# Self-attention stage of a Perceiver kernel: value product with its operands swapped, one output product, row sums in two steps

## The chip, the cores and the metric

The kernel runs on one core of one Trainium2 chip. Its measure is the device time of one execution in microseconds (us), as the median of several runs. The engines of the core are TensorE (PE in the profile; PEld is its weight load), VectorE (DVE), ScalarE (ACT), GpSimd (POOL) and SyncE (SP), which here only starts transfers.

## What is computed

Inputs: x is 128 batches x 32 queries x 128 channels, the context 128 x 257 x 128. Everything is float32. Three blocks follow one another, each added to its input:

```
x = x + cross_attention(layernorm(x), ctx, ctx, mask)        # 16 heads of 8 channels
x = x + self_attention(layernorm(x))
x = x + mixture_of_experts(layernorm(x))                      # 4 layers, 4 experts, the best 2
```

The change is in the second:

```
qkv    = x @ W_qkv + b_qkv                       # B, N = 128, 32
energy = einsum('bqhe,bkhe->bqhk', q, k)
attn   = softmax(energy, axis=-1) / sqrt(128)
out    = einsum('bihv,bvhd->bihd', attn, v)
return out.reshape(B, N, 128) @ W_out + b_out
```

Each softmax row has 32 entries, the positions of one batch.

## The kernel before, in words

The program has three stages, each a block in which every engine has its own written list of instructions, with semaphores between them. Stage 1 is the cross attention (the first 492 us), stage 2 the self attention (492 to 637 us), stage 3 the experts (the rest).

**Stage 2.** The 4096 tokens are 32 tiles of 128 (four batches of 32 tokens), and 8 blocks of four tiles. A step works on one block, and in it four places w = 0 to 3 each work on one tile of each of five phases, side by side: at place w of step s, scores are made for tile 4s+w+2 (`sc`), row sums for tile 4s+w+1 (`nm`), the transpose for tile 4s+w (`tr`), the value product for the tile before (`pv`), and the output product for the one before that (`y`). Beside them, the projections of block s+2 (`f`) are spread over the places: at w = 0 its normalised tokens `xm` are transposed, at w = 1 and 2 its queries and keys are projected, at w = 3 its values. The heads stand as 4 groups (G) of 4 (GH).

The order in which each engine takes the work of one place is fixed by the program text:

- TensorE: scores (L1279), projection (L1287, L1292 or L1295), transpose (L1302), value product (L1314), output product (L1322).
- VectorE: row maximum (L1226), difference (L1229), at w = 3 the normalising of block s+3 (L141), at w = 1 and 2 the low half of queries or keys (L1239), row sum (L1244), reciprocal (L1246), output added to `xs` (L1250), its statistics (L1254).
- ScalarE: the copy of the projection out of PSUM (L1164, L1173, L1177), the transposed probabilities `pT` (L1182), the value product `oT` (L1187), the exponential (L1195).
- GpSimd: at w = 0 the bias added to a block of `xs` (L1145), then the probabilities times the reciprocals (L1150).
- SyncE starts the transfers: it places the values V2 (L164), writes the queries and keys of a block to DRAM (L148) and its values (L152), and then reads queries (L157) and keys (L160) back in the layout of the scores, and last loads two parts of the experts' weights (L1121, L1122). The scores at w = 2 are the first of a new block and wait for these reads.

Waits that the prediction uses: the low halves of the queries have to be done (`c_lo`) before the keys are projected, as both go through one PSUM bank:

```python
                            if f and w in (1, 2):
                                pe.wait_ge(c_xTc, f.n + 1)
                                wait(pe, c_lo, 2 * f.n + w - 1)
```

The value product puts the four heads of a group on the partitions, so its output holds for every head the columns of all heads, of which only its own are wanted; four copies of W_out (`WoutM`), each with the rows of the other heads at zero, pick them in four output products that add up. These copies are made by VectorE in `prepare` at the start of stage 2, with `bv2R` (the value bias, scaled), the last six layer-norm deviations, and `boutR`.

**Stage 1** is a list of slots s from -22 to 133, one batch each. At s = 2 it loads the weights of the self attention; from FIRST = 113 it already makes the projections of the first block.

## Time and profile before

| | |
|---|---|
| median of 3 runs | 1492.02 us (1490.94 to 1494.69) |
| the profiled execution: its own time, and its span | 1491.5 us, 1489.3 us |
| granted TensorE clock, mean over the span | 0.957 |
| busy over the span: TensorE, VectorE, ScalarE, GpSimd | 89%, 82%, 74%, 47% |
| stage 2, of the span | 492 to 637 us |

The span runs from the first to the last instruction. Engine times in the profile are busy times of an engine, and each row names the line of the kernel, the engine, the tile written and the tiles read. A timeline row begins with the start of the instruction and its duration, both in us.

### The profile page before, as it was taken

To read this page: it belongs to the slowest core of one execution; us is meant where nothing else is said; L and a number is where in the kernel's file an instruction comes from. 1 tells how busy PE (TensorE), PEld (TensorE's weight loads), DVE (VectorE), ACT (ScalarE), POOL (GpSimd) and SP (SyncE) were. 2 spreads that over 40 slices of the span, in tenths; PEclk is the share of its full clock that TensorE was granted. 3 is DMA by queue.
4 is the path that set the end of the run, shared out by engine and by line. 5 is a ranking of instruction groups with operands and counts; after the bars stand their busy time and mean duration, and the time that the engine had idled before them with its cause. 6 is when DMAs were issued, how large, how long until landed. Compare 5 with 4: busy or idle time off the path is not lost.

```text
span 1489.3 us, 46126 instructions
## 1 busy us (share of the span) xinstructions
PE 1326.8 (89%) x15863; PEld 1010.5 (68%) x15863; DVE 1217.0 (82%) x3478; ACT 1101.6 (74%) x1844; POOL 702.9 (47%) x464
## 2 busy tenths in 40 slices
PE   5898999999978699969887898999999999898988
PEld 3676777777857599936665666766676666666666
DVE  6799999998997788778788777787877878787885
ACT  2698999999978255538777677777787778677776
POOL 7276777777768433223332233443444344333323
PEclk9999999999987599979999899999999999999999
DMA  5975766666642478400000000000000000000000
GB/s 154 233 194 158 190 178 185 187 172 188 180 135 65 122 195 198 112 1 2 2 0 0 0 1 2 0 0 0 0 0 0 0 0 0 2 7 14 7 14 15
DMA packets 196200, 108.46 MB, mean 73 GB/s; under 512 B 89740, under 2 KB 194028, under 8 KB 196076
## 3 DMA queue, kind: packets, MB, share of 16 engines
q1 hardware_dynamic: 122032, 84.65, 20.4%
q10 hardware_dynamic: 74044, 22.17, 6.8%
q8 instruction: 76, 1.25, 0.4%
q14 instruction: 48, 0.39, 0.1%
HBM read 67.62 MB, written 39.03 MB: 72 GB/s over the span
## 4 chain that ended last, share of the span: by engine, by line
DVE 20%; PE 14%; issue 13%; ACT 5%; DVEq 2%; ACTq 0%
PE pair L1734 7%; PE pair L1716 5%; DVE hs L1647 4%; ACT gf L1589 3%; ACT gh L1594 2%; DVE xc L1621 2%; DVE gl L1633 1%; DVE rs L50 1%; DVE rs L52 1%; DVE st L1612 1%; PE pair L1746 1%; DVE rs L48 1%; DVE rs L37 1%; DVE mv L1616 1%; DVE sel L1699 1%
## 5 line engine op out<-in xcount | busy, mean ns | idle before, releaser
L1576 POOL TENSOR_TENSOR gl<-gf,gh 128x1024 f16<-128x1024 f32 x128 | 292.6, 2286 | 543.9 <-ACT gh L1594 543.9
L1589 ACT ACTIVATE gf<-pair,b1c 128x512 f32<-128x512 f32 x512 | 326.6, 679 | 149.1 <-PE pair L1716 148.9
L1734 PE MATMUL pair<-w2p,gh 128*128 (+1 forms) x4096 | 366.9, 222 | 12.0 <-DVE gl L1633 12.0
L1734 PE MATMUL pair<-w2p,gl 128*128 (+1 forms) x2048 | 358.1, 222 | 0.0
L1734 PEld LDWEIGHTS pair<-w2p,gh 128*128 128x128 f16 x4096 | 326.5, 99 | 37.7 <-issue 8.4
L407 POOL TENSOR_TENSOR pl<-p,ph 128x1024 f16<-128x1024 f32 x128 | 272.7, 2131 | 125.5 <-ACT ph L464 125.2
L1716 PE MATMUL pair<-xh,w1p 128*128 128x512 f16 x1024 | 327.1, 381 | 3.6 <-DVE w2p L1363 2.9
L1594 ACT ACTIVATE gh<-gf 128x1024 f16<-128x1024 f32 x256 | 270.6, 1057 | 25.2 <-ACT gf L1589 2.0
L1633 DVE TENSOR_TENSOR gl<-gf,gh 128x1024 f16<-128x1024 f32 x128 | 169.0, 1320 | 122.7 <-ACT gh L1594 120.6
L1734 PEld LDWEIGHTS pair<-w2p,gl 128*128 128x128 f16 x2048 | 203.5, 99 | 0.0
L1716 PE MATMUL pair<-xl,w1p 128*128 128x512 f16 x512 | 195.0, 381 | 0.0
L463 ACT ACTIVATE p<-pair 128x512 f32<-128x512 f32 x256 | 158.8, 620 | 32.6 <-PE pair L868 31.1
L1716 PEld LDWEIGHTS pair<-xh,w1p 128*128 (+1 forms) x1024 | 100.6, 98 | 111.8 <-issue 5.0
L464 ACT ACTIVATE ph<-pair 128x512 f16<-128x512 f32 x256 | 161.2, 630 | 0.0
L770 DVE TENSOR_REDUCE mx<-pair 128x4 f32<-128x1024 f32 x128 | 154.7, 1208 | 1.3 <-PE pair L841 0.2
L1647 DVE SCALAR_TENSOR_TENSOR hs<-pair,comb,hs 128x128 f32 (+1 forms) x512 | 142.6, 337 | 6.9 <-PE pair L1734 6.9
L891 PE MATMUL pair<-VX,ph 128*128 128x36 f16 x1024 | 92.5, 180 | 7.9 <-DVE lsb L608 5.1
L891 PEld LDWEIGHTS pair<-VX,ph 128*128 128x128 f16 x1024 | 84.1, 97 | 18.8 <-issue 14.8
L841 PE MATMUL pair<-KS,QS 97*128 97x256 f16 x512 | 79.4, 278 | 14.7 <-DVE mx L770 13.3
L892 PE MATMUL pair<-VX,ph 128*128 128x36 f16 x1024 | 91.8, 180 | 0.0
L893 PE MATMUL pair<-VX,pl 128*128 128x36 f16 x1024 | 91.8, 180 | 0.0
L821 PE MATMUL pair<-cT,WkT 128*128 128x512 f32 x128 | 72.0, 645 | 19.1 <-DVE VX L797 9.2
(232 smaller groups left out, 2518.8 us busy)
## 6 DMA issues: line engine op xcount, KB each, us to landing
KS<-k_parts_dram SPq DMA_DIRECT2D x64, 384.0 KB, 4.5
k_parts_dram<-kh SPq DMA_DIRECT2D x64, 256.0 KB, 3.3
cx<-in_ctx_dram ACTq DMA_DIRECT2D x30, 512.0 KB, 4.4
k_parts_dram<-kl SPq DMA_DIRECT2D x64, 128.0 KB, 3.5
w1p<-in_L_ffn_w_dram SPq DMA_DIRECT2D x8, 512.0 KB, 6.1
w2p<-in_L_ffn_w_dram SPq DMA_DIRECT2D x8, 512.0 KB, 8.0
QS<-q_parts_dram ACTq DMA_DIRECT2D x128, 24.0 KB
Q<-q_parts_dram SPq DMA_DIRECT2D x32, 96.0 KB
```

What stands on the lines that cost most here:

```text
L407: pool.tensor_tensor(pl[n % 4][:, :, :], p32[n % 2][:, :, :], ph[n % 4][:, :, :], ALU.subtract).then_inc(pl_done, 1)
L463: act.activation(p32[n % 2][:, c, :], TB[:, c * 512:(c + 1) * 512], ACT.Exp)
L464: act.activation(ph[n % 4][:, c, :], TB[:, c * 512:(c + 1) * 512], ACT.Exp).then_inc(t_read[c], 1)
L770: dve.tensor_reduce(mx[n // PB % 2][:, :, n % PB], RB[:, :].rearrange("p (g k) -> p g k", g=G), AX.X, ALU.max).then_inc(r_read, 1)
L891: pe.matmul(o, p_hi, hi, start=(c == 0), stop=False)
L1576: pool.tensor_tensor(gl[u.m2][:, 0:h, :], gf[u.m2][:, 0:h, :], gh[u.m2][:, 0:h, :], ALU.subtract).then_inc(d_loP, 1)
L1589: act.activation(gf[u.m2][:, c, :], hb[c][:, :], ACT.Gelu, scale=1.0 / WS, bias=b1c[:, u.step.expert(u.e), c]).then_inc(d_g, 1)
L1594: act.activation(gh[u.m2][:, c - 1:c + 1, :], gf[u.m2][:, c - 1:c + 1, :], ACT.Copy).then_inc(d_hi, 1)
L1633: dve.tensor_tensor(gl[u.m2][:, h:FC, :], gf[u.m2][:, h:FC, :], gh[u.m2][:, h:FC, :], ALU.subtract).then_inc(d_loD, 1)
L1647: dve.scalar_tensor_tensor(t, yb[v.m2][:, k * D:(k + 1) * D], comb[v.step.m2][:, k, v.e:v.e + 1], t, ALU.mult, ALU.add).then_inc(d_acc, 1)
L1716: last = pe.matmul(hb[c][:, :], w1p[:, u.step.expert(u.e), part, c * P:(c + 1) * P].rearrange("p a f -> p (a f)"), x[k][u.step.m2][:, :], ...
L1734: last = pe.matmul(yb[v.m2][:, t * D:(t + 1) * D], g[:, c, t * P:(t + 1) * P], w2p[:, le, part, c, :].rearrange("p a h -> p (a h)"), start ...
```

## The change

It has four parts.

- The value product takes the transposed probabilities as weights and V2 as the moving operand. Its output has queries and heads on the partitions and (group, head, channel) along the row. ScalarE copies it whole (`of`); GpSimd then takes, for each of the four heads of a group, the quarter of 32 partitions and of its own channels and multiplies it by the reciprocal row sums (`on2`, four instructions a tile); VectorE transposes the 128 x 128 result in 32 x 32 squares (`oT2`). One output product with the whole of W_out takes the place of four.
- The probabilities are no longer multiplied by the reciprocals, and the transpose on TensorE waits for the exponential alone. The row sum is made in two steps: GpSimd adds the right half of each row of 32 to the left half (`hs2`), VectorE sums the 16 columns left.
- The normalising of block s+3 moves from VectorE to ScalarE, with scale `rs2` and bias `nb2` (a new small VectorE product, twice in the program).
- `WoutM`, `rowsel` and `sel3` go. W_out is loaded in another order of rows, by four transfers (four more for the value bias in place of one), and scaled by ScalarE in stage 1, as is `bv2R`; the product of the value bias and its sum with `boutR` also move to stage 1.

```diff
@@ stage 1, SyncE, s == 2
-                        sp.dma_start(Wout[:, :], W_out).then_inc(c_w, 16)
+                        for j in range(GH):
+                            sp.dma_start(Wout[GD * j:GD * (j + 1), :],
+                                         W_out.rearrange("(g j d) n -> j g d n", j=GH, d=DH)[j]).then_inc(c_w, 16)
+                            sp.dma_start(bv2_c[GD * j:GD * (j + 1), :],
+                                         b_qkv[2 * D:3 * D].rearrange("(g j d a) -> j g d a", j=GH, d=DH, a=1)[j]).then_inc(c_w, 16)
...
@@ stage 1, ScalarE
+                    if s == FIRST - 4:
+                        act.wait_ge(c_w, CW)
+                        act.activation(Wout[:, :], Wout[:, :], ACT.Copy, scale=float(D) ** -0.5).then_inc(c_wm, 1)
+                        act.activation(bv2R[:, :], bv2_c[:, 0:1].broadcast_to((P, D)), ACT.Copy).then_inc(c_wm, 1)
...
@@ stage 1, VectorE
                     if s == FIRST - 2:
...
+                        dve.scalar_tensor_tensor(nb2[:, 0:EARLY], mv2[:, 0:EARLY, 0], -1.0, rs2[:, 0:EARLY], ALU.mult, ALU.mult).then_inc(c_ln, 1)
...
+                    if s == FIRST + 5:
+                        dve.wait_ge(c_w, CW)
+                        dve.wait_ge(c_b, 1)
+                        dve.tensor_tensor(boutR[:, :], WB[0][:, 0:D], boutR[:, :], ALU.add).then_inc(c_wm, 1)
...
@@ stage 1, TensorE
+                    if s == FIRST + 4:
+                        pe.wait_ge(c_wm, 2)
+                        pe.wait_ge(c_vn, 1)
+                        pe.matmul(WB[0][:, 0:D], bv2R[:, :], Wout[:, :], start=True, stop=True).then_inc(c_b, 1)
...
@@ stage 2, GpSimd
                             if f and w == 0:
 
-                                pool.wait_ge(c_wm, 6)
+                                pool.wait_ge(c_wm, 3)
+                                wait(pool, c_on, GH * (4 * st.s - 1))
+                                wait(pool, c_hf, 4 * st.s + 1)
...
                             if nm is not None:
                                 i = (w + 1) % 4
-                                pool.wait_ge(c_rc, nm + 1)
-                                pool.tensor_tensor(pr[i][:, :, :, :], pr[i][:, :, :, :],
-                                                   rc2[i][:, :, :].unsqueeze(3).broadcast_to((P, PB, G, SQ)),
-                                                   ALU.mult).then_inc(c_nrm, 1)
+                                pool.wait_ge(c_exp, nm + 1)
+                                wait(pool, c_on, GH * (nm - 2))
+                                wait(pool, c_sum, nm - 1)
+                                pool.tensor_tensor(hs2[(w + 1) % 2][:, :, :, :], pr[i][:, :, :, 0:SQ // 2], pr[i][:, :, :, SQ // 2:SQ],
+                                                   ALU.add).then_inc(c_hf, 1)
+                            if pv is not None:
+                                i, r = (w + 1) % 2, (w - 1) % 4
+                                pool.wait_ge(c_rc, pv + 1)
+                                pool.wait_ge(c_oc, pv + 1)
+                                pool.wait_ge(c_bias, f.n + 1 if f else NBLK)
+                                pool.wait_ge(c_hf, NT if nm is None else nm + 1)
+                                wait(pool, c_oT, pv - 1)
+                                for h in range(GH):
+                                    own = slice(SQ * h, SQ * (h + 1))
+                                    pool.tensor_tensor(on2[i][own, :, :, :], of[i][own, :, :, h, :],
+                                                       rc2[r][own, :, :].unsqueeze(3).broadcast_to((SQ, PB, G, DH)),
+                                                       ALU.mult).then_inc(c_on, 1)
...
@@ stage 2, ScalarE
+                            if w == 3 and st.block(3):
+                                b = st.block(3)
...
+                                wait(act, c_xT, b.n)
+                                for k in range(4):
+                                    t = bass.ds(4 * b.n + k, 1)
+                                    act.activation(xm[:, k, :], xs[:, t, :].rearrange("p a c -> p (a c)"), ACT.Identity,
+                                                   scale=rs2[:, t], bias=nb2[:, t]).then_inc(c_xm, 1)
...
                             if pv is not None:
                                 i = (w + 1) % 2
                                 act.wait_ge(c_o, pv + 1)
-                                wait(act, c_y, pv - 1)
-                                act.activation(oT2[i][:, :, :, :].rearrange("p h b q -> p b h q"),
-                                               bank[6][:, :].rearrange("p (b h q) -> p b h q", b=PB, h=GH),
+                                wait(act, c_on, GH * (pv - 1))
+                                act.activation(of[i][:, :, :, :, :].rearrange("p b g h d -> p (b g h d)"), bank[6][:, :],
                                                ACT.Copy).then_inc(c_oc, 1)
...
@@ stage 2, VectorE
                     def prepare():
-                        dve.tensor_scalar(bv2R[:, :], bv2_c[:, 0:1].broadcast_to((P, D)), float(D) ** -0.5, None, ALU.mult).then_inc(c_wm, 1)
-                        for j in range(GH):
-
-                            dve.tensor_scalar(WoutM[:, j, :], Wout[:, :], rowsel[:, j:j + 1], float(D) ** -0.5,
-                                              ALU.mult, ALU.mult).then_inc(c_wm, 1)
...
-                        dve.wait_ge(c_b, 1)
-                        dve.tensor_tensor(boutR[:, :], bank[7][:, 0:D], boutR[:, :], ALU.add).then_inc(c_wm, 1)
+                        dve.scalar_tensor_tensor(nb2[:, late], mv2[:, late, 0], -1.0, rs2[:, late], ALU.mult, ALU.mult).then_inc(c_ln, 1)
...
-                            if w == 3 and st.block(3):
-                                normalise(st.block(3))
...
-                                dve.wait_ge(c_exp, nm + 1)
-                                dve.tensor_reduce(sm2[i][:, :, :], pr[i][:, :, :, :], AX.X, ALU.add).then_inc(c_sum, 1)
+                                dve.wait_ge(c_hf, nm + 1)
+                                wait(dve, c_on, GH * (nm - 3))
+                                dve.tensor_reduce(sm2[i][:, :, :], hs2[(w + 1) % 2][:, :, :, :], AX.X, ALU.add).then_inc(c_sum, 1)
                                 dve.wait_ge(c_sum, nm + 1)
                                 dve.reciprocal(rc2[i][:, :, :], sm2[i][:, :, :]).then_inc(c_rc, 1)
+                            if pv is not None:
+                                i = (w + 1) % 2
+                                dve.wait_ge(c_on, GH * (pv + 1))
+                                wait(dve, c_y, pv - 1)
+                                dve.transpose(out=oT2[i][:, :, :].rearrange("p b q -> p (b q)"),
+                                              in_=on2[i][:, :, :, :].rearrange("p b g d -> p (b g d)")).then_inc(c_oT, 1)
...
@@ stage 2, TensorE
                             if tr is not None:
-                                pe.wait_ge(c_nrm, tr + 1)
+                                pe.wait_ge(c_exp, tr + 1)
...
                                     last = pe.matmul(bank[6][:, b * P:(b + 1) * P],
+                                                     pT[(w + 1) % 2][:, b * P:(b + 1) * P],
                                                      V2[m][:, t * PB + b, :, :].rearrange("k g c -> k (g c)"),
-                                                     pT[(w + 1) % 2][:, b * P:(b + 1) * P], start=True, stop=True)
+                                                     start=True, stop=True)
...
                             if y is not None:
-                                pe.wait_ge(c_oc, y + 1)
+                                pe.wait_ge(c_oT, y + 1)
                                 wait(pe, c_yr, y)
-                                for h in range(GH):
-                                    last = pe.matmul(bank[7][:, 0:D], oT2[w % 2][:, h, :, :].rearrange("p b q -> p (b q)"),
-                                                     WoutM[:, h, :], start=(h == 0), stop=(h == GH - 1))
-                                last.then_inc(c_y, 1)
+                                pe.matmul(bank[7][:, 0:D], oT2[w % 2][:, :, :].rearrange("p b q -> p (b q)"), Wout[:, :],
+                                          start=True, stop=True).then_inc(c_y, 1)
```

## Rows read from the trace of the kernel before

**Rows 1.** Windows, one step: length, PE, PEld, DVE, ACT, POOL, clock, DMA share, GB/s.
```profile
525.00:541.30 16.30, 16.30 (x163) 15.03 (x162) 13.64 (x31) 9.13 (x17) 5.43 (x5) 1.00 0.74 194
```

**Rows 2.** Timeline of TensorE, one place (w = 1) and the next steps' scores.
```profile
561.59 1.11 PE L1279 MATMUL pair<-K,Q 96*128 96x32 f16 x16
...
562.55 1.10 PE L1292 MATMUL pair<-xmT,Wqkv 128*128 128x512 f32 x2
...
563.49 0.60 PE L1302 MATMUL pair<-ident,pr 128*128 128x128 f32 x4
...
563.93 1.06 PE L1314 MATMUL pair<-pT,V 128*128 128x128 f32 x8
...
564.82 1.06 PE L1322 MATMUL pair<-WoutM,oT 128*128 128x128 f32 x8
...
565.72 1.11 PE L1279 MATMUL pair<-K,Q 96*128 96x32 f16 x16
...
577.84 1.12 PE L1279 MATMUL pair<-K,Q 96*128 96x32 f16 x16
```

**Rows 3.** Timeline of VectorE in the same place (w = 1).
```profile
562.74 0.69 DVE L1226 TENSOR_REDUCE mx<-pair 128x16 f32<-128x512 f32 x1
...
563.46 0.69 DVE L1229 TENSOR_TENSOR dif<-pair,mx 128x512 f32<-128x512 f32 x1
...
565.17 0.68 DVE L1244 TENSOR_REDUCE sm<-pr 128x16 f32<-128x512 f32 x1
...
566.07 0.29 DVE L1250 TENSOR_TENSOR xs<-pair,xs 128x128 f32 x1
...
566.50 0.29 DVE L1254 BATCH_NORM_STATS2 st<-xs  x1
```

**Rows 4.** Timeline of place w = 3: value projection, its copy, normalising, next copy.
```profile
570.80 1.14 PE L1295 MATMUL pair<-Wqkv,xmT 128*128 128x128 f32 x8
...
572.06 0.60 ACT L1177 ACTIVATE vn<-pair 128x512 f32<-128x512 f32 x1 [1.80 <-PE pair L1295]
...
572.32 1.11 DVE L141 TENSOR_SCALAR xm<-xs,mv,rs 128x128 f32 x4
572.55 0.59 ACT L1182 ACTIVATE pT<-pair 128x512 f32<-128x512 f32 x1
```

**Rows 5.** Instructions near to the new ones, by line: duration min/median/max in ns.
```profile
L1150 POOL TENSOR_TENSOR pr<-pr,rc x32: 1046/1047/1052, 509.5 to 628.9; 128x512 f32<-128x512 f32 x32
...
L415 POOL TENSOR_TENSOR tl<-VL,plast x32: 432/442/465, 66.2 to 480.4; 128x144 f32<-128x144 f32 x32
...
L1145 POOL TENSOR_TENSOR xs<-xs,boutR x8: 1262/1270/1278, 502.0 to 591.7; 128x512 f32<-128x512 f32 x4, 128x512 f32 x4
...
L652 DVE STREAM_TRANSPOSE onT<-on x64: 220/230/247, 78.7 to 490.1; 128x64 f32<-128x64 f32 x64
```

**Rows 6.** Timeline, stage 3: sixteen ScalarE instructions of the new kind, in one run.
```profile
651.83 6.25 ACT L1407 ACTIVATE hs<-xs,nb,rs 128x128 f32<-128x128 f32 x16
```

**Rows 7.** Timeline of the start of stage 2.
```profile
493.44 5.57 DVE L1207 TENSOR_SCALAR WoutM<-Wout,rowsel 128x128 f32<-128x128 f32 x4
...
498.03 0.69 ACT L1173 ACTIVATE qkh<-pair,bqk_c 128x512 f16<-128x512 f32 x1 [2.17 <-PE pair L1292]
...
501.75 0.74 DVE L1239 SCALAR_TENSOR_TENSOR qkl<-pair,bqk_c,qkh 128x512 f16<-128x512 f32 x1
...
502.64 2.04 PE L1292 MATMUL pair<-xmT,Wqkv 128*128 128x512 f32 x2 [3.71 <-DVE qkl L1239]
```

**Rows 8.** Timeline: key loads, waiting scores; page: issues of a like load.
```profile
510.85 0.36 SPq L160 DMA_DIRECT2D K<-k_parts_dram  x1
...
516.75 1.17 PE L1279 MATMUL pair<-K,Q 96*128 96x32 f16 x16 [0.51 <-DMA K<-k_parts_dram]
...
574.91 0.36 SPq L160 DMA_DIRECT2D K<-k_parts_dram  x1
...
KS<-k_parts_dram SPq DMA_DIRECT2D x64, 384.0 KB, 4.5
```

More of the change, by code:

```diff
@@ L94, in build @@
         ident16 = sb(whole, "ident16", [P, P], F16)
-        rowsel = sb(whole, "rowsel", [P, GH], F32)
         boR = sb(whole, "boR", [P, D], F32)
@@ L102, in build @@
         bv2_c = sb(whole, "bv2_c", [P, 1], F32)
+        bv2R = sb(whole, "bv2R", [P, D], F32)
+        c_wm, c_b = sem("c_wm"), sem("c_b")
+        CW = 16 * (4 + 2 * GH)
         boutR = sb(whole, "boutR", [P, D], F32)
@@ L109, in build @@
         mv2 = sb(whole, "mv2", [P, NT, 2], F32)
-        rs2, rw2, rt2 = (sb(whole, f"rs2_{i}", [P, NT], F32) for i in range(3))
+        rs2, rw2, rt2, nb2 = (sb(whole, f"rs2_{i}", [P, NT], F32) for i in range(4))
         xm = sb(whole, "xm", [P, 4, D], F32)
@@ L1018, in build @@
             NBLK = NT // 4
-            WoutM = sb(S, "WoutM", [P, GH, D], F32)
-            bv2R = sb(S, "bv2R", [P, D], F32)
             qkh = [qkh[0], [sb(S, f"qkh1{k}", [P, 4 * P], F16) for k in range(2)]]
```

58 lines of the change are left out of this document (22 added, 36 removed).

## The prediction

> **What bounds it now.** I read the windows first. The self-attention stage takes 145 us of the span, from 492 to 637, and in its middle a step of four tiles takes 16.3 us in which TensorE is busy all the time, at the full granted clock (1.0, the 2.4 GHz level), VectorE for 84%, ScalarE 56%, GpSimd 33% [rows 1]. So TensorE bounds this part, and the other stages see the change only in small edits. The timeline then shows what one place consists of. From start to start: scores 0.96, projection 0.94, transpose 0.44, value product 0.89, output product 0.90, together 4.13 us, and the next place begins [rows 2]. At w = 0 the short transposes of `xm` stand in for a projection, so that four places make 577.84 - 561.59 = 16.25 us. VectorE's place runs maximum, difference, [low half], row sum, reciprocal, addition, statistics [rows 3], and ends ahead of TensorE's. Its lead is what the change spends.
>
> **The output product** goes from four to one: 3/4 of 0.90 = 0.67 us a tile off the engine that bounds, and 16.25 - 4 x 0.67 = 13.6 us a step, if TensorE went on without a pause. The value product keeps its shape with the operands swapped: nothing.
>
> **VectorE** loses the normalising (1.11 us a step [rows 4]) and half of each row sum. The row sum is 0.68 for 512 elements [rows 3], a transpose 0.23 for 64 [rows 5]: about 1.0 ns an element, so half a row sum is 0.42. It gains the transpose. At 128 elements that is some 0.30, and 0.24 from start to start, as an instruction starts up to 0.08 before the last one's end. In the order maximum, difference, row sum, reciprocal, transpose, addition, statistics, from start to start, a place then costs it 0.72 + 0.61 + 0.44 + 0.24 + 0.24 + 0.43 + 0.22 = 2.9 us, and 0.67 more at w = 1 and 2: 12.9 a step, under 13.6.
>
> **GpSimd** loses 1.05 us a tile and gains a half sum and four quarters. Multiplications take 1.047 us for 512 elements and 0.442 for 144 [rows 5]: 1.64 ns an element on a fixed 0.205. A quarter has 128 elements a row: 0.415. The half sum has 256: 0.63, or with the slower addition of L1145 (1.27 for 512) up to 0.77; I take 0.70. What four quarters take together, which I call T, no row shows. From above: one after another, 4 x 0.415 = 1.66. From below: all side by side, each on its own 32 partitions, little over 0.5. I take the fixed parts one after another and one element part, 4 x 0.205 + 0.21 = 1.03, as instructions on separate partitions need not share the work by element but do share the way into the engine. Between the ends 0.5 and 1.66 that is the middle, and both ends stay in the range.
>
> The Trainium skill's page GPSIMD Engine Reference, section Instruction dispatch, says that each core of the engine serves its own 16 partitions and starts the next instruction as soon as its own share is done. By it the quarters overlap, and T would lie at or under my value. No row of before has GpSimd instructions on parts of the partitions that could show it.
>
> **The new waits** are what decides. VectorE's transpose stands in its queue behind the reciprocal and waits for GpSimd's quarters, these for ScalarE's copy `of`, that for the value product of the same place. Behind the waiting transpose queue the addition, the statistics, and the next place's maximum, difference and low half; and TensorE may not project the keys before the low half of the queries (L1291). The second new load is on ScalarE at w = 3: four normalising instructions, between the copy `vn` and `pT` and `of`. Sixteen like them took 6.25 us [rows 6], so four take 1.6, and `of` comes that much later. GpSimd then still has the bias (1.24) before the next quarters, at w = 0. This closes a ring once a step. From the start of the value projection: to `vn` 1.26 [rows 4], `vn` 0.49, normalising 1.6, `pT` 0.49, `of` 0.65 with the signal, quarters T, bias 1.24, half sum 0.70, quarters T + 0.05, transpose 0.24, addition 0.43, statistics 0.22, maximum 0.72, difference 0.61 [rows 3], low half 0.75 [rows 7] + 0.05, keys' projection 0.94, transpose 0.44, value product 0.89, output product 0.23, scores 0.96 [rows 2]. The sum is 12.96 + 2T. With T = 1.03 a step lasts 15.0 us, not 13.6; with T = 1.66 it lasts 16.3, as now.
>
> A second ring runs through the transfers: from the first scores of a block (565.72) to `vn` (572.06) 6.34, less 0.67 for one output product; from there to the issue of the key load at 574.91 2.85; to its landing 4.5, as for stage 1's load of the same size, up to 5.9, as the scores at 516.75 waited for a load issued at 510.85 [rows 8]. That is 13.0 to 14.4. It sits close under the first ring, and the DMA share, 0.74 of 16.3 us [rows 1], becomes 0.8.
>
> **The sum.** Five full steps (blocks 2 to 6) at 16.25 - 15.0 = 1.2: -6.2 us. The start of the stage: `WoutM` holds VectorE 5.6 us, and the low half that was due at 498.77, when `qkh` ended, begins at 501.75, with TensorE idle 3.7 for it [rows 7]. Between the end of `WoutM` at 499.0 and that low half lie 2.7 us of small instructions; with `WoutM` gone they are over by 497, and the low half begins when due: -3.0, and the transpose no longer waits for GpSimd's product, -0.2. The last eight tiles have no projections: 4.13 - 0.94 = 3.2 us a place now, bound by VectorE's 2.9 afterwards: -2.4, less 1.0 for the longer way out after the last value product (quarters, transpose): -1.4. Stage 1 gets two copies on ScalarE (0.39 each by rows 6), `nb2` (some 0.2), one addition on VectorE (0.29) and one small product: 0 to 1.9, and I take +0.8, as these engines are dense there. The six more transfers at s = 2 come far ahead of their use, and SyncE's loads of keys run slots ahead: nothing. Together -6.2 - 3.2 - 1.4 + 0.8 = -10.0. The profiled execution took 1491.5 us (span 1489.3 and 2.2 around it), so 1481.5; the median of the runs is 0.5 above it: 1482.0.
>
> Another rule that bears on GpSimd's new work is in SBUF — State Buffer of the Trainium skill, section Who interferes with whom: a VectorE instruction with one SBUF input outside the two-port modes does not contend with GpSimd. The new sum and transpose are of that kind. If it failed, they would wait out each half sum, 0.7 us a tile, and the step would be 16 us or more.
>
> **Rivals.**
> - *The quarters run one after another.* T = 1.66, ring 16.3: the steps give nothing. Left are -3.2 at the start, -0.8 at the end (a way out 0.6 longer), +0.8: -3.2, 1488.8 us, within 0.3%. For it: consecutive instructions on all partitions show no overlap worth naming. Against: those share all partitions.
> - *GpSimd becomes a loss.* One mechanism: an instruction on 32 partitions with eight-element runs costs 0.6 us, T = 2.4, the ring 17.8: five steps at +1.5, -3.2, +0.3 at the end, +0.8: +5.4, 1497.4 us. It decides from T = 1.7 a step, and over the whole from about 2.0. The dearest comparable row, L1145, would make a quarter 0.5 (T = 2.0) [rows 5].
> - *TensorE stays the bound.* T near 0.5 puts the ring at 14.0, the transfers at 13.0 to 14.4; with both at their lower end 13.6 to 14.0 a step: five steps at -2.4, -3.2, -1.7, +0.4: -16.5, 1475.5 us.
> - *The output product does not matter*, because steps are held by the transfers: landing at 5.9 under more load, 14.4 or more, and SyncE's issues late. The time is near my forecast; only the wait is another.
>
> **Chances.** Forecast, with the fourth rival: 0.55 (1478 to 1486). One after another: 0.23. Loss: 0.10. TensorE bound: 0.08. The rest, 0.04, is a wait I haven't seen, most likely a loss. A measurement of this kernel can tell 0.3%, 4.5 us. Faster by more (under 1487.5): 0.55 + 0.08 + a third of the second: 0.70. Within 0.3%: 0.18. Slower: 0.12. The range, 1475 to 1490.5, leaves out the loss and little else.
>
> **What would show it.** The output product's row at a quarter of its count, TensorE busy some 90% of a step instead of all of it. Steps of 15.0 us in the starts of the scores, four places apart. The wait of VectorE's transpose for GpSimd, longest after w = 3; TensorE waiting for the low half before the keys' projection and for VectorE's addition before the output product. The four quarters' length from first start to last end: under 1.0 confirms the forecast or better, 1.6 the first rival, 2.0 the second. First scores of a block waiting for the key load would show the fourth. At the start, the second projection some 3 us sooner. I am wrong if steps stay at 16.2 with T near 1, if GpSimd's instructions lengthen VectorE's, or if stage 1 grows by more than 2 us.

## The result, and the profile after

The changed kernel took 1516.8 us (median of 4, 1514.3 to 1519.8) against 1492.4: a ratio of 1.016, 95% interval 1.014 to 1.019. I had said 1482.0, and faster at 0.70. The profiled execution took 1519.8 us (span 1518.0), 28.7 more than before's span. The starts of three instructions, each from its row by line, split that: the maximum of stage 1, that of stage 2, and stage 3's first hidden product. I put my terms beside them. Each difference is one profiled execution against one.

| part of the span | before | after | difference | my term |
|---|---|---|---|---|
| start to first maximum of stage 1 | 36.1 | 41.5 | +5.4 | 0 |
| to its last maximum | 426.9 | 428.1 | +1.2 | +0.8 |
| to stage 2's first, and its first four tiles | 54.9 | 55.4 | +0.5 | -3.2 |
| five steps (525.0 to 611.3) | 81.3 | 86.3 | +5.0 | -6.2 |
| last tiles, to the first hidden product | 68.2 | 68.0 | -0.2 | -1.4 |
| stage 3's hidden products, first to last | 811.2 | 828.5 | +17.3 | 0 |
| the rest | 10.6 | 10.2 | -0.4 | 0 |

Windows of one step after (columns as in [rows 1]):
```profile
541.82:559.26 17.44, 15.83 (x140) 14.18 (x139) 12.09 (x31) 10.81 (x22) 10.60 (x21) 0.90 0.72 185
```
Against [rows 1] TensorE has become an engine with gaps, VectorE is busy for 12.1 us (12.9 forecast), and GpSimd has doubled. A step takes 86.3 / 5 = 17.26 us; before 16.27. Groups by line in stage 2 (busy, mean ns | idle before, releaser):
```profile
L1173 POOL TENSOR_TENSOR on<-of,rc 32x128 f32<-32x128 f32 x128 | 51.3, 401 | 44.9 <-ACT of L1219 28.4 <-DVE rc L1267 6.4 <-POOL hs L1162 1.9
L1162 POOL TENSOR_TENSOR hs<-pr 128x256 f32<-128x256 f32 x32 | 23.5, 735 | 4.8 <-ACT pr L1226 2.3
L1343 PE MATMUL pair<-Wout,oT 128*128 128x128 f32 x64 | 14.3, 307 | 14.2 <-DVE xs L1277 14.2
L1265 DVE TENSOR_REDUCE sm<-hs 128x16 f32<-128x256 f32 x32 | 13.1, 410 | 2.2 <-POOL hs L1162 1.9
L1209 ACT ACTIVATE xm<-xs,rs,rs 128x128 f32 (+1 forms) x28 | 11.5, 483 | 7.3 <-PEq L295 7.3
L1272 DVE STREAM_TRANSPOSE oT<-on 128x128 f32<-128x128 f32 x32 | 10.0, 312 | 33.3 <-POOL on L1173 33.3
```
The single instructions came out as sized: quarter 0.401 us (0.415), half sum 0.735 (0.70), row sum 0.410 (0.42). The two waits I named are there: VectorE's transpose for GpSimd, 33.3 us over 32 tiles, and the output product for VectorE's addition. What I had wrong is how four quarters add up. Timeline of GpSimd, ScalarE, VectorE and TensorE around w = 3:
```profile
597.34 1.64 ACT L1209 ACTIVATE xm<-xs,rs,rs 128x128 f32 x4
598.89 0.58 ACT L1214 ACTIVATE pT<-pair 128x512 f32<-128x512 f32 x1
599.37 0.58 ACT L1219 ACTIVATE of<-pair 128x512 f32<-128x512 f32 x1
600.16 1.83 POOL L1173 TENSOR_TENSOR on<-of,rc 32x128 f32<-32x128 f32 x4 [2.09 <-DVE rc L1267]
602.02 0.31 DVE L1272 STREAM_TRANSPOSE oT<-on 128x128 f32<-128x128 f32 x1 [1.88 <-POOL on L1173]
602.12 1.27 POOL L1155 TENSOR_TENSOR xs<-xs,boutR 128x512 f32<-128x512 f32 x1
602.33 0.29 DVE L1277 TENSOR_TENSOR xs<-pair,xs 128x128 f32 x1
602.77 0.46 PE L1343 MATMUL pair<-Wout,oT 128*128 128x128 f32 x2 [1.55 <-DVE xs L1277]
603.35 0.75 POOL L1162 TENSOR_TENSOR hs<-pr 128x256 f32<-128x256 f32 x1
604.35 1.82 POOL L1173 TENSOR_TENSOR on<-of,rc 32x128 f32<-32x128 f32 x4 [0.26 <-POOL hs L1162]
606.20 0.31 DVE L1272 STREAM_TRANSPOSE oT<-on 128x128 f32<-128x128 f32 x1 [1.21 <-POOL on L1173]
```
This is my ring, link by link: normalising, `pT`, `of`, quarters, bias, half sum, quarters, transpose. Four quarters take 1.83 us from first start to last end: no overlap at all, and 0.07 between each pair. (The first bracket names `rc`, but the reciprocals of this tile had been made two places earlier; the quarters waited for `of`, which ended at 599.95.) The ring's sum with T = 1.83 is 12.96 + 3.66 = 16.6. Part of what it lacks stands in these rows: from `of` to the quarters 0.79 us (I had 0.65), from the first quarters to the bias 1.96 (T is 1.83), and from the half sum to the next quarters 1.00 (0.70 and 0.05).

**The start.** VectorE and GpSimd, 25 to 37 us, first in the kernel before:
```profile
27.76 2.91 POOL L382 MEMSET VX<- 128x640 f16 x1
28.52 2.24 DVE L742 CAST ident<-ident 128x128 f16<-128x128 f32 x1
30.27 0.41 POOL L383 MEMSET sel<- 128x16 f32 x1
30.76 0.27 POOL L385 TENSOR_SCALAR_AFFINE_SELECT sel<-sel 128x16 f32<-128x16 f32 x1
31.37 3.51 POOL L391 MEMSET Q<- 96x4096 f32 x1
```
and after:
```profile
27.35 2.90 POOL L386 MEMSET VX<- 128x640 f16 x1
28.10 7.38 DVE L747 CAST ident<-ident 128x128 f16<-128x128 f32 x1
29.83 3.83 POOL L387 MEMSET Q<- 96x4096 f32 x1
33.59 1.81 POOL L388 MEMSET V<- 128x2048 f32 x1
```
Before, VectorE's cast ends at 30.76, between the selector's memset and its first select, which waits for that memset: the short `sel3` instructions, with the waits between them, let it through. Without them each of three memsets begins before the one ahead has ended (29.83 against 30.25), and the cast is held until 35.5.

**Stage 3**, VectorE's normalisation `xc` and GpSimd's low half `gl`, a quick block and the next, a slow one:
```profile
1014.03 1.12 DVE L1641 TENSOR_SCALAR xc<-hs,mv,rs 128x128 f32 x4
1014.93 3.35 POOL L1596 TENSOR_TENSOR gl<-gf,gh 128x1024 f16<-128x1024 f32 x1 [3.14 <-ACT gh L1614]
1015.21 0.66 PE L1766 MATMUL pair<-ident,xc 128*128 128x128 f32 x4 [1.03 <-DVE xc L1641]
...
1038.07 3.01 DVE L1641 TENSOR_SCALAR xc<-hs,mv,rs 128x128 f32 x4
1038.87 2.13 POOL L1596 TENSOR_TENSOR gl<-gf,gh 128x1024 f16<-128x1024 f32 x1 [3.05 <-ACT gh L1614]
1041.13 1.12 PE L1766 MATMUL pair<-ident,xc 128*128 128x128 f32 x4 [3.02 <-DVE xc L1641]
...
1090.07 3.44 POOL L1596 TENSOR_TENSOR gl<-gf,gh 128x1024 f16<-128x1024 f32 x1 [3.05 <-ACT gh L1614]
```
If `gl` begins 0.90 us after `xc`, it is the one held; at 0.80, the fourth `xc`, which starts 0.77 us after the first, is held for 1.9 us. It is a race: in block 17 `gl` began 0.81 after `xc` (last row) and `xc` still won, as `gl`'s 3.44 us show. From one block's `xc` to the next is 24.0 us in the first case, 27.2 in the second. Windows of the two blocks:
```profile
1014.03:1038.07 24.04, 23.01 (x261) 16.50 (x260) 19.16 (x63) 19.07 (x27) 9.76 (x4) 1.00 0.00 0
1038.07:1065.23 27.16, 24.14 (x261) 17.63 (x260) 20.56 (x62) 18.99 (x27) 8.54 (x4) 0.94 0.00 0
```
So the 3.1 us more have two parts. TensorE waits 3.02 us for `xc` and not 1.03, 2.0 more; and from the end of that wait or just behind it the granted clock, 1.00 all through the quick block, is at half (1.2 GHz) for 3.4 us, TensorE being busy 1.1 us longer with the same 261 instructions. Every slow block has such a spell. Blocks 11 to 24 hold six slow ones (27.1 to 28.7 us) after, none (23.9 each) before: 22 us, of which blocks 4 to 10, 5 us shorter than before, give some back.

The Trainium skill's page SBUF — State Buffer, section Who interferes with whom, says that VectorE's copies, casts and tensor_scalars may take a port pair which they share with GpSimd, and that whoever comes first shuts the other out for the whole instruction. Both places agree with it (the cast held for 7.38 us, the fourth `xc` for 1.9); I had used that section for the new instructions of stage 2 alone, where it held too (row sum 0.410, transpose 0.312).

### The profile page after: what moved, and what is told of

It reads as the page before. It is cut to its first block, busy times and chain, and to the rows that moved or that the text cites. A ratio compares the mean times of both kernels' runs of the same rounds, so it can differ in the third digit from the quotient of the medians.

```text
span 1518.0 us, 46101 instructions
## 1 busy us (share of the span) xinstructions
PE 1328.8 (88%) x15671; PEld 1006.3 (66%) x15671; DVE 1213.2 (80%) x3478; ACT 1114.1 (73%) x1874; POOL 736.9 (49%) x589
## 4 chain that ended last, share of the span: by engine, by line
DVE 20%; PE 15%; issue 12%; ACT 5%; DVEq 1%; ACTq 0%
PE pair L1754 7%; PE pair L1736 6%; DVE hs L1667 4%; ACT gf L1609 3%; DVE xc L1641 2%; ACT gh L1614 2%; DVE rs L50 1%; DVE gl L1653 1%; DVE rs L52 1%; PE pair L1766 1%; DVE st L1632 1%; DVE rs L48 1%; DVE rs L37 1%; DVE mv L1636 1%; PE pair L1743 1%
## 5 line engine op out<-in xcount | busy, mean ns | idle before, releaser
L1596 POOL TENSOR_TENSOR gl<-gf,gh 128x1024 f16<-128x1024 f32 x128 | 285.8, 2233 | 568.1 <-ACT gh L1614 568.1
L1754 PE MATMUL pair<-w2p,gh 128*128 (+1 forms) x4096 | 373.1, 224 | 12.1 <-DVE gl L1653 12.1
L1754 PE MATMUL pair<-w2p,gl 128*128 (+1 forms) x2048 | 363.8, 223 | 0.0
L1754 PEld LDWEIGHTS pair<-w2p,gh 128*128 128x128 f16 x4096 | 330.8, 100 | 38.5 <-issue 9.5
L1653 DVE TENSOR_TENSOR gl<-gf,gh 128x1024 f16<-128x1024 f32 x128 | 163.9, 1280 | 126.7 <-ACT gh L1614 124.6
L893 PE MATMUL pair<-VX,ph 128*128 128x36 f16 x1024 | 92.4, 180 | 10.6 <-DVE lsb L608 5.2
```

What stands on the lines that cost most here:

```text
L893: pe.matmul(o, p_hi, hi, start=(c == 0), stop=False)
L1596: pool.tensor_tensor(gl[u.m2][:, 0:h, :], gf[u.m2][:, 0:h, :], gh[u.m2][:, 0:h, :], ALU.subtract).then_inc(d_loP, 1)
L1653: dve.tensor_tensor(gl[u.m2][:, h:FC, :], gf[u.m2][:, h:FC, :], gh[u.m2][:, h:FC, :], ALU.subtract).then_inc(d_loD, 1)
L1754: last = pe.matmul(yb[v.m2][:, t * D:(t + 1) * D], g[:, c, t * P:(t + 1) * P], w2p[:, le, part, c, :].rearrange("p a h -> p (a h)"), start ...
```

## The experiments

Steps are the starts of stage 2's maxima, from the fifth to the 25th tile, divided by five; stage 3 is from first to last hidden product; `xc` its mean. Medians are of 4 to 10 runs beside as many or more of the kernel before (1489.7 to 1491.2).

| run | median us | ratio, 95% | step us, clock there | stage 3 us | `xc` ns |
|---|---|---|---|---|---|
| before | | | 16.27, 1.00 | 811.2 | 355 |
| changed | 1516.8 | 1.014-1.019 | 17.26, 0.90 | 828.5 | 445 |
| 1 fillers | 1509.8 | 1.012-1.016 | 17.20, 0.90 | 825.6 | 431 |
| 2 late transpose | 1507.0 | 1.009-1.012 | 16.98, 0.92 | 823.2 | 416 |
| 3 one multiply | 1494.9 | 0.999-1.004 | 14.45, 1.00 | 819.8 | 416 |
| 4 bias later | 1508.3 | 1.008-1.014 | 16.96, 0.89 | 824.9 | 430 |
| 5 selector last (before) | 1495.7 | 1.001-1.004 | 16.27, 1.00 | 811.8 | 355 |
| 6 stage 3 later (before) | 1503.3 | 1.006-1.010 | 16.30, 1.00 | 822.3 | 356 |
| 7 normalise on VectorE | 1512.9 | 1.009-1.018 | 19.10, 0.85 | 814.1 | 370 |
| 8 reordered, first | 1510.6 | 1.009-1.016 | 18.26, 0.88 | 826.1 | 429 |
| 9 normalise earlier | 1492.0 | 1.000-1.003 | 16.72, 0.96 | 805.9 | 356 |
| 10 TensorE kept busy | 1517.2 | 1.014-1.024 | 17.33, 0.98 | 826.9 | 444 |
| 11 reordered, second | 1477.3 | 0.989-0.993 | 15.02, 1.00 | 807.2 | 355 |
| 12 reordered, third | 1478.3 | 0.991-0.994 | 15.90, 0.95 | 806.3 | 356 |
| 13 full multiply | 1493.3 | 1.001-1.004 | 17.50, 0.98 | 806.9 | 356 |
| 14 second, one multiply | 1468.7 | 0.982-0.987 | 14.67, 1.00 | 807.5 | 356 |
| 15 stage 3 kept apart | 1562.6 | 1.046-1.051 | 17.04, 0.92 | 874.7 | 342 |
| 16 second, kept apart | 1545.8 | 1.034-1.040 | 14.75, 1.00 | 878.0 | 343 |
| 17 small op first | 1571.4 | 1.049-1.056 | 17.24, 0.90 | 881.9 | 686 |
| 18 second, small op first | 1540.6 | 1.031-1.036 | 15.03, 1.00 | 875.7 | 681 |

**The start: runs 1 and 5.** Run 1 puts the selector's instructions back:
```diff
+                pool.memset(sel3[:, :, :], 1.0).then_inc(a_fill, 1)
...two affine selects with their waits, ahead of Q2's memset
```


> The changed kernel with the three small GpSimd instructions that made the row selector (memset and two affine selects, 128x16 each) put back between the memset of VX and those of Q2 and V2; nobody reads their result. Theory: the changed kernel loses 5.4 us in its first 42 us, because VectorE's copies into the 16-bit identity and wo_p (2.2 us before, 7.3 us after) are held up while GpSimd's memsets follow one another without a gap; the three small instructions gave VectorE its gap. Then the first running maximum of stage 1 comes back from 41.5 us to about 36.1 us, and the time falls from 1516.8 to about 1511.5 us, give or take what stage 3 does with the shift. Rival: the start grew for another reason (loads, the order of the queues), and the time stays within 1 us of 1516.8.

> The kernel before with one thing moved: the three small GpSimd instructions that make the row selector come after the memsets of Q2 and V2 and not before them, as if they weren't there for those who wait at that point. Theory: the gap that they leave between GpSimd's memsets is what lets VectorE's copies through; without it the first maximum of stage 1 moves from 36.1 us to about 41.5 us, and the time grows by about 5.4 us or, if stage 3 is sensitive to when it begins, by up to 20 us. Rival: the order of memsets doesn't matter, the first maximum stays at 36 us and the time at 1490.4.

First maximum at 35.9 us in run 1; 41.0 in run 5, whose median is 5.0 us over its neighbours' of before. Both theories held: 5 us of the loss come from three tiny instructions, and the waits between them, that went.

**The ring: runs 3, 2 and 4.** Run 3:
```diff
-                                for h in range(GH):
-                                    own = slice(SQ * h, SQ * (h + 1))
+                                for h in range(1):
+                                    own = slice(0, P)
```


> The changed kernel with one GpSimd multiplication over 128 partitions (the first quarter of each row, 128x128) in place of the four over 32; it leaves out three of four diagonal quarters of the value product, and so computes something else. Theory: the four instructions run one after another (0.40 us each, 1.83 us together), and one takes 0.4 to 0.7 us; a step falls from 17.3 us to between 13.6 and 14.5 us, where TensorE or the transfers take over, and the time to about 1497 us. Rival: the steps are set by something other than the quarters (ACT's normalising, the split row sum, the transpose): the steps stay above 16 us and the time above 1508.

Its row by line (ns min/median/max):
```profile
L1173 POOL TENSOR_TENSOR on<-of,rc x32: 405/408/410, 521.0 to 622.5; 128x128 f32<-128x128 f32 x32
```
128 partitions take as long as 32. T falls by 1.83 - 0.41 = 1.42, and my ring, which holds T twice, asks for 2.84 us a step; measured 17.26 - 14.45 = 2.81. That fits my ring's slope, its constant 0.64 short both times (16.62 for 17.26, 13.78 for 14.45), but the agreement to 0.03 is in part luck. A step of run 3:
```profile
541.20:555.60 14.40, 14.05 (x138) 12.53 (x138) 11.60 (x31) 10.40 (x21) 5.81 (x9) 1.00 0.85 230
```
TensorE is busy 14.05 of 14.40 us there, so the ring hardly sets this step any more. What is shown is that the quarters are in the ring of the changed kernel, and are worth at least 2.8 us of its step.

Run 2 moves the transpose behind the next place's difference, run 4 the bias behind the quarters.

> The changed kernel with VectorE's transpose of a tile moved behind the running maximum and difference of the next place, so that GpSimd's four quarters (1.83 us together) have a whole place to finish in. Theory: the quarters stand in the ring that sets the step, value product, ACT's eviction, quarters, transpose, addition, statistics, next maximum; with the transpose later the step falls from 17.3 us to about 15.0, the granted clock in stage 2 rises from 0.85 towards 1.0, and the time falls by 10 to 14 us, to about 1505. Rival: GpSimd's own order (bias addition, half sum, quarters) holds the place at w=0 whatever VectorE does, steps stay above 16.5 and the time falls by 4 us at most.

> The changed kernel with GpSimd's addition of the output bias (1.27 us, once in a step at w=0) moved behind the four quarters of its place. Theory: in that place GpSimd runs bias, half sum and quarters without a gap, with VectorE's transpose waiting at their end, so the step falls by 0.8 to 1.25 us, to about 16.3, and the time by 4 to 6 us, to about 1511.5. Rival: the place only shifts its wait to the next one, and the time falls by less than 1.5 us.

Steps of 16.98 and 16.96: each alone gives 0.3 us, far under what I expected. In both, ScalarE's 1.6 us still delays the quarters of w = 3; in run 2 the half sum that waits behind bias and quarters then holds VectorE up to 2.0 us.

**The normalising: runs 7, 8 and 9.** Run 7 gives it back to VectorE, behind the difference; run 8 joins runs 1, 2, 4 and moves it behind the exponential of w = 3; run 9 changes the changed kernel by this alone:
```diff
-                            if w == 3 and st.block(3):
+                            if w in (1, 2) and st.block(3):    # placed behind the exponential
...
-                                for k in range(4):
+                                for k in (2 * w - 2, 2 * w - 1):
```


> The changed kernel with the normalisation of a block (four 128x128) back on VectorE (1.1 us) from ACT (1.64 us). Theory: on ACT it stands ahead of the eviction of the transposed probabilities and of the value product in the place w=3, and so delays the quarters there by 1.5 us; on VectorE it only takes 1.1 us at a point where that engine would wait for GpSimd: the step falls from 17.3 us to 15.8 to 16.5, and the time by 4 to 8 us. Rival: VectorE has no such room, the step stays within 0.3 us of 17.3 and the time within 2 us.

> The changed kernel with four moves together: fillers back between GpSimd's memsets, VectorE's transpose in the next place, GpSimd's bias addition behind the quarters, and ACT's normalisation behind the exponential of its place. The same instructions, in another order. Theory: each of the moves takes one piece of work out of the ring that sets the step; together the step falls from 17.3 us to 14 to 14.6 us, the clock in stage 2 stays at 1.00, and the time is 1483 to 1490 us with stage 3 in its slow course (825 us) and 1470 to 1476 with the quick one (811 us). Rival: the four quarters hold the step by themselves (GpSimd busy 4 times 2.6 us and 1.3 us, 11.7 us in a step, but always behind ACT's eviction), steps stay above 16 us and the time above 1500.

> The changed kernel with ACT's normalisation of the next block (four of 0.48 us at w=3, ahead of both evictions) moved behind the exponentials of w=1 and w=2, two tiles in each. Theory: in the changed kernel TensorE waits about 1.5 us once in a step, at w=3, because ACT's 1.6 us stand ahead of the two evictions there, the quarters start that much later and everything behind them too; after that wait the granted clock falls to half for 3.4 us, which costs as much again. Without it the step falls from 17.3 us to 14.5 to 15.8 and stage 2's clock rises from 0.90 to 0.95 or more; time 1503 to 1511. Rival: the 1.6 us only move to another place (as when they were put behind the exponential of w=3, where TensorE then waited 1.6 us for them), and the step stays above 16.8.

Run 7's theory and run 8's fell: steps of 19.1 and 18.3 us. In both TensorE waits for the normalised block at w = 0, in run 8 1.6 us each time (group of its transposes):
```profile
L1316 PE MATMUL pair<-ident,xm 128*128 128x128 f32 x20 | 4.2, 344 | 8.1 <-ACT xm L1233 8.1
```
Early enough, in run 9, the same instructions give 0.5 us a step, not the 1.5 to 2.8 that I expected, 2.5 in the last tiles (25.7 to 23.3), and a quick stage 3. The median falls by 25 us. The profiled execution, the fastest of the ten, is 33 us shorter than the changed kernel's, 22.6 of them in stage 3.

**Is it the clock? Run 10.**
```diff
+                            if f and w == 3:
+                                pe.wait_ge(c_lo, 2 * f.n + 2)
+                                for b in range(6):
+                                    pe.transpose(bank[1][:, (b % 4) * D:(b % 4 + 1) * D], xmT[:, (b % 4) * P:(b % 4 + 1) * P], ident[:, :])
```


> The changed kernel with six further TensorE transposes (128x128 of xmT into a bank that is free there, about 0.22 us each, 1.3 us together, nobody reads them) between the value product and the output product of w=3, where TensorE otherwise waits about 1.5 us. Theory: it is the wait that brings the granted clock down to half for 3.4 us in each step; with work in its place the clock stays at 1.00 in stage 2 and, though TensorE has 1.3 us more to do in a step, the step falls from 17.3 us to 15.5 to 16.5 us. Rival: the clock doesn't follow from that wait, or the slow 3.4 us cost nothing since the ring through GpSimd sets the step: the step stays at 17.3 us or grows.

The clock came back to 0.98 and the step stayed at 17.33: the rival. In the changed kernel TensorE waits 1.3 to 1.7 us in each of the five steps, and behind it the granted clock drops to half (1.2 GHz) for 3.4 us, but in stage 2 that time is hidden: the ring through GpSimd is what lasts. The wait isn't at w = 3, as I had written, but at w = 0, ahead of the output product (602.77 in the rows above). There run 10's transposes only make TensorE come later, and it still waits 0.7 to 1.4 us. Behind it, where the changed kernel works at half clock, run 10 mostly has the full clock, and waits 0.8 us at w = 1 and 0.9 at w = 2 (none, and at most 0.5, in the changed kernel). Its extra transposes, 0.8 us, are work that the changed kernel hasn't, so it bounds what the clock costs and doesn't measure it.

**A better order: runs 11 to 14.** Run 11 is run 8 with run 9's normalising; run 12 the same with the bias ahead of the quarters. Run 14 is run 11 with one multiplication, run 13 with one over 128 x 512 and four transposes:
```diff
+                                pool.tensor_tensor(on2[i][:, :, :, :, :].rearrange("p b g h d -> p (b g) (h d)"), of[i]..., rc2[r]..., ALU.mult)
...
+                                for h in range(GH):
+                                    last = dve.transpose(out=oT2[i][own, :, :]..., in_=on2[i][own, :, :, h, :]...)
```


> The changed kernel with fillers between GpSimd's memsets, VectorE's transpose in the next place, GpSimd's bias addition behind the quarters, and ACT's normalisation behind the exponentials of w=1 and w=2. It differs from the first reordered kernel in the place of the normalisation alone. Theory: that kernel's step of 18.3 us came from TensorE's waiting 1.6 us for the normalised block and the clock dips behind it; here nothing in the ring is left that needs more than TensorE's 13.6 us, the step is 13.8 to 14.8 us with the clock at 1.00, and the time 1470 to 1488 us, by the course of stage 3. Rival: TensorE waits somewhere else, dips stay, and the step stays above 16 us.

> As the second reordered kernel, but with GpSimd's bias addition left ahead of half sum and quarters at w=0. Theory: with the transpose in the next place, GpSimd's 1.3 us at w=0 still delay the quarters of that place, VectorE's transpose behind them and the half sum: the step is 0.3 to 1.3 us longer than in the second reordered kernel. Rival: there is enough slack by now and the two steps agree within 0.2 us.

> The second reordered kernel with one GpSimd multiplication of 128x128 (0.41 us) in place of the four; it leaves out three of four diagonal quarters, and so computes something else. Theory: with everything else out of the ring, the four instructions still hold the step at 15.0 us, and without 1.4 us a tile it falls to what TensorE has to do, 13.6 to 14.0 us. Rival: what holds the 15.0 us is the way of queries, keys and values through memory: the step stays within 0.4 us of 15.0.

> The second reordered kernel (1477.3 us, step 15.0 us) with GpSimd's four quarter multiplications replaced by one over all 128 partitions and 512 columns, and VectorE's one transpose by four over 32 partitions that take the quarters. Theory: a GpSimd instruction's time follows its columns, not its partitions (0.40 us for 32x128, 0.41 for 128x128), so one of 128x512 takes 1.05 us against 1.83 for the four, and four transposes of 32 partitions take 0.25 to 0.6 us more on VectorE than the one: the step falls by 0 to 0.8 us, time 1473 to 1477. Rival: VectorE's four transposes take as long each as the one (0.31 us, 1.2 together), its 0.9 us more in a place take up what GpSimd saves, and the step grows by up to 1 us.

Run 11 takes 15.0 us a step, a little over what I expected, and 1477.3 us: 0.991 of the kernel before, with the change's own instructions. Run 12's step is 0.9 longer. Run 14, which computes something else, shows that the quarters have left the ring: 0.35 us less, not 2.8, and the same stage 2 gave 14.75 and 15.03 in runs 16 and 18. What holds 14.7 us was not isolated, but run 14's trace has the sign of its rival: the five steps alternate between 14.0 and 15.0 to 15.4 us, and the one wait of TensorE over 1 us in two of the long ones (1.1 and 1.5) is for the key load. Windows of 20 tiles of run 11:
```profile
517.10:592.20 75.10, 71.84 (x684) 63.39 (x685) 60.91 (x151) 52.04 (x98) 51.39 (x102) 0.98 0.84 211
```
Run 13's rival held, and more: a transpose of 32 partitions takes 0.300 us, as long as one of 128, and the step grew by 2.5 us where the rival had up to 1.
```profile
L1266 DVE STREAM_TRANSPOSE oT<-on 32x128 f32<-32x128 f32 x80 | 24.0, 300 | 0.8
L1170 POOL TENSOR_TENSOR on<-of,rc 128x512 f32<-128x512 f32 x20 | 21.0, 1048 | 42.7 <-DVE oT L1266 26.1 <-ACT of L1217 16.6
```

**Stage 3: runs 6, 15 to 18.** Run 6 puts eight VectorE instructions between the stages of the kernel before. Runs 15 and 16 add a wait in stage 3, runs 17 and 18 a small instruction:
```diff
+                            if f and e == 0:
+                                pool.wait_ge(d_x, 4 * f.n + 4)          # runs 15, 16
...
+                            if f and e == 0:                            # runs 17, 18
+                                pool.tensor_tensor(spare[:, :], gf[u.m2][:, 0, 0:64], gh[u.m2][:, 0, 0:64], ALU.subtract)
```


> The kernel before, with eight further VectorE instructions (128x128, about 0.34 us each, some 2.7 us together) between stage 2 and stage 3, written to a tile that nobody reads; stages 1 to 3 themselves are untouched. The changed kernel's stage 3 is 17 us longer than before's (first to last hidden product 828.5 us against 811.2) though its code is the same. Theory: stage 3 has a quick and a slow course, in the slow one VectorE's normalisation xc meets GpSimd's low half gl again and again and TensorE's clock dips every 51 us, and which course it takes hangs on the instant at which it begins; then this kernel's stage 3 also comes out at 815 to 830 us and the time rises by clearly more than the 2.7 us put in, to 1495 to 1510. Rival: stage 3 is slower for something that the change leaves behind (the place of tiles in memory, the activation unit's state): stage 3 stays at 811 us and the time at 1490 to 1493.5.

> The changed kernel with one wait more, in stage 3: at the first expert of a block GpSimd starts its low half gl only when VectorE has finished the normalisation xc of the next block. Stages 1 and 2 are the changed kernel's. Theory: stage 3's slow blocks (27.2 us against 23.9) are those in which VectorE's xc is held for 1.9 us by GpSimd's gl, after which TensorE waits and its clock falls to half for 3.4 us; kept apart, the blocks 11 to 24 all take 23.9 us, stage 3 takes 806 to 812 us against 828, and the time falls from 1516.8 to about 1500 us. Rival: the held xc is a consequence of the clock's dips and not their cause, or the added wait delays GpSimd's own work: stage 3 stays at 820 us or more.

> The second reordered kernel with the same wait in stage 3. Its profiled stage 3 already ran in the quick course (807.2 us, no block above 24 us among blocks 11 to 24). Theory: nothing to gain there, the time stays within 3 us of 1477.3 us. Rival: blocks 4 to 9 (28 to 31 us each) are lengthened by the same meeting of the two engines, and the time falls by 5 us or more.

> The changed kernel with one small GpSimd subtraction more (128x64, about 0.2 us, result unused) in stage 3, ahead of the low half gl of a block's first expert. In a slow block of the changed kernel GpSimd's gl begins 0.80 us after VectorE's xc and holds its last instruction for 1.9 us; in a quick one it begins 0.89 us after it and is itself held until VectorE is done. Theory: this tenth of a microsecond decides between 23.9 and 27.2 us; with the small instruction in front, VectorE loses 0.2 us at most, no block of 11 to 24 takes over 25 us, stage 3 takes 806 to 815 us and the time falls from 1516.8 to 1497 to 1504 us. Rival: the held xc only accompanies a slow block whose cause is elsewhere, or the small instruction is met in the same way: stage 3 stays at 820 us or more, the time above 1510.

> The second reordered kernel (1477.3 us) with the same small GpSimd subtraction in stage 3. Theory: its stage 3 is in the quick course already; the small instruction costs nothing that can be measured, time within 3 us of 1477.3. Rival: blocks 4 to 9 (28 to 31 us) get shorter too and the time falls by 5 us or more; or GpSimd's 0.2 us delay the output product and stage 3 grows by over 3 us.

Run 6: unchanged code of the kernel before, begun a little later, has a stage 3 of 822 us. So its length isn't fixed by its code, as the theory said. Run 6 also adds a tile, which its rival would blame; but run 9 and the changed kernel have the same tiles and the same stage 3, at 805.9 and 828.5 us, which leaves how it is entered as the likelier reason. In run 6 `xc` is not held (356 ns), and the blocks that grew, the 9th to 11th and the 25th, did so otherwise. Runs 15 and 16 went against me. They cost 46 and 68 us against the kernels that they change (the changed one and run 11): `xc` is never held (342), but `gl` then comes late for TensorE, which waits 2.3 us for it, and from the 10th block on nearly all take 27 to 29 us. Runs 17 and 18 cost 55 and 63 us against the same two: the small instruction wins GpSimd the race in every block from the 10th on.
```profile
L1644 DVE TENSOR_SCALAR xc<-hs,mv,rs 128x128 f32 (+1 forms) x128 | 79.7, 686 | 1.2
```
686 - 342 = 344 ns in the mean of four is 1.4 us a block, and all blocks from the 10th on take 27.2 to 29.0 us. That is the slow block of the changed kernel, made on demand: a held `xc`, or a `gl` late by as much, is worth some 3.3 us of a 23.9 us block, and in these runs too each such block has its 3.4 us or more at half clock. The half clock that was hidden in stage 2 is part of the loss here; how much the wait would cost without it no run tells.

## Why the prediction was wrong

**GpSimd's quarters.** The step that failed first is "I take the fixed parts one after another and one element part ... = 1.03". T is 1.83, above the first rival's 1.66 by the gaps. With the two T of the ring that is +1.6 us a step, 8 us over five. The row on which I might have leaned was my own rival's: consecutive instructions show no overlap. The rule that I cited for overlap, in the Trainium skill's GPSIMD Engine Reference, Instruction dispatch, isn't borne out for four instructions on separate quarters, which start 0.47 us apart; memsets of the same kernel do start up to 0.42 us before the one ahead has ended.

**The ring.** Right in its links (the rows around w = 3), 0.64 us short a step, 3 us; its slope fits run 3, with the luck said there. With T = 1.83 it gives 16.6, a little more than the old step: the first rival nearly, and on steps alone a loss of 2 us, not of 5.

**ScalarE at w = 3.** I priced its 1.6 us inside the ring (measured 1.64) and was right that it lies there. I missed that it could stand elsewhere, for 0.5 us a step (run 9).

**The start of stage 2.** My -3.2 is +0.5, though the gain that it stood for came true. Stage 1's last product before, the same after, and the second projection after:
```profile
490.41 0.80 PE L901 MATMUL pair<-WoT,onT 128*128 128x128 f32 x2 [1.94 <-DVE onT L652]
...
498.69 0.79 PE L903 MATMUL pair<-WoT,onT 128*128 128x128 f32 x2 [1.94 <-DVE onT L652]
507.87 2.04 PE L1313 MATMUL pair<-xmT,Wqkv 128*128 128x512 f32 x2 [0.72 <-DVE qkl L1259]
```
From that product to the second projection it was 12.2 us before (502.64 in [rows 7]) and 9.2 after: the 3.0 that I forecast. But stage 1's way from its last maximum to that product took 1.7 us more, and stage 2's first four tiles, already in the ring, 1.8 more. The first of these may be chance: in runs 15 and 17, whose stages 1 and 2 are the changed kernel's, stage 2's first maximum comes another 2 us sooner. **The last tiles**: -1.4 became -0.2. **Stage 1**: +0.8, measured +1.2; but that stretch varies from 426.6 to 429.9 us between profiles of the same code (runs 15 and 17), so the term is neither shown nor refuted.

**What no term had.** The sentence "the other stages see the change only in small edits" failed. `sel3` goes, which I priced at nothing without looking who runs beside it: +5.4 us, shown by runs 1 and 5. And stage 3 was taken as fixed: +17.3 us. That a held `xc` or a late `gl` makes slow blocks is shown by runs 15 and 17; that stage 3's length hangs on more than its own code and tiles, by runs 6 and 9. Single kernels whose runs spread from 1492.3 to 1514.1 us (run 4) fit that, but only one execution of each was profiled. Which kernel gets which course isn't settled. All kernels with four ScalarE instructions at w = 3 and no addition in stage 3 (the changed one, runs 1 to 4, 8, 10) had it at 819.8 us or more, those with them elsewhere (5, 7, 9, 11 to 14) at 806 to 814; why, no run tells.

So of 28.7 us, 5.4 are the start, some 5 the steps, 17.3 stage 3. The medians differ by 24.4 us only. Without stage 3's part the change would have cost 7 to 11 us: the sign was wrong even so.

## What to carry to other kernels

Before pricing a removed GpSimd instruction at nothing, look at which VectorE copies, casts or tensor_scalars run beside it: a gap between GpSimd's instructions can be the only moment at which they get through. Cutting one GpSimd or VectorE operation into four by partitions cost about four times the time here, not the same. What a spell at half clock costs depends on what sets the length of the stage: hidden behind another ring in stage 2, part of the loss in stage 3. When work moves to another engine, try its place in that engine's order before judging the move: the same instructions in another order, with the three fillers back, made 1517 us into 1477.

## What I had not expected of the hardware

- GpSimd: 32 x 128 takes 0.401 us and 128 x 128 0.408; four of the former on separate quarters 1.83. VectorE's transpose: 0.300 us for 32 x 128, 0.312 for 128 x 128.
- A VectorE cast of 128 x 128 took 7.38 us beside three GpSimd memsets without a gap; a copy of the same size behind it in the kernel before took 0.21.
- A tenth of a microsecond between `xc` and `gl` (0.80 against 0.90) went with blocks of 27.2 and 24.0 us in all but one of fourteen.
- Half clock for 3.4 us in each step of stage 2 changed next to nothing in its length (17.33 us without it but with 0.8 us more work for TensorE, 17.26 with it); in stage 3 every slow block has such a spell.
